# Edges sorted by destination block and source group, seven-chunk picks, and ranks made by TensorE, in a four-layer graph network on one core

## The reference

```python
# layer 0, twice: relational messages, summed by destination
W = jnp.einsum('rb,bio->rio', a, V)                  # 20 types out of 8 bases
agg = segment_sum(x[src], dst * R + etypes, N * R).reshape(N, R, -1)
h = jnp.einsum('nri,rio->no', agg, W) + x @ w_loop + bias
# layer 1: sum of the sources' rows
out = segment_sum(x[src], dst, N)
# layer 2: two small networks on every edge; their results are summed at the
# destination (forward) and at the source (backward), then a third per node
flow_f = mlp(cat(x[dst], x[src], edge_attr));  total_f = segment_sum(flow_f, dst, N)
flow_b = mlp(cat(x[src], x[dst], edge_attr));  total_b = segment_sum(flow_b, src, N)
x = mlp(cat(total_f, total_b))
# layer 3: attention with 4 heads of 8, softmax over the edges of a destination
scores = (q[dst] * k[src]).sum(-1) / sqrt(8);  out = segment_softmax(scores) * v[src] ...
```

## Time and profile before

| | before |
|---|---|
| time, median of 3 runs | 4352.77 us (4341.38 to 4362.70) |
| profiled execution | span 3621.4 us; no whole time is recorded for it |
| median minus span | 731.4 us |
| TensorE / VectorE / GpSimd / ScalarE busy | 72% / 71% / 62% / 16% |
| mean TensorE clock granted | 0.801 of full |
| instructions | 58407 |

### The profile page before, as it was taken

One profiled execution on the slowest core, in us unless ns is written; L12 is line 12 of the kernel. 1 busy time (PEld: TensorE's weight loads), 2 busy tenths in 40 slices (PEclk: granted clock), 3 DMA queues, 4 the chain that ended last, 5 costly groups with the idle time before them and its releaser, 6 DMA issues. The chain is left out here.

```text
span 3621.4 us, 58407 instructions
## 1 busy us (share of the span) xinstructions
PE 2609.3 (72%) x19499; PEld 1755.0 (48%) x19499; DVE 2555.5 (71%) x7445; ACT 577.7 (16%) x1352; POOL 2259.7 (62%) x2253
## 2 busy tenths in 40 slices
PE   0600000999998999977889799999999967777751
PEld 0400000777776777764555466666666543333331
DVE  9400000998874988869999677777777559999987
ACT  0100000000001000000011122222222213333320
POOL 2777776877762777747777355555555357777750
PEclk9555555788885888878889799999999968888885
DMA  6300001111113111111111100000000011111120
GB/s 96 103 8 8 8 8 58 31 23 24 25 12 103 25 23 24 24 17 28 26 27 26 12 10 10 11 10 10 10 11 10 6 24 27 27 27 27 27 19 5
DMA packets 125028, 91.67 MB, mean 25 GB/s; under 512 B 59542, under 2 KB 110678, under 8 KB 124118
## 3 DMA queue, kind: packets, MB, share of 16 engines
q0 software_dynamic: 70912, 41.10, 7.7%
q1 hardware_dynamic: 53846, 46.89, 5.3%
HBM read 60.42 MB, written 27.41 MB: 24 GB/s over the span
## 5 line engine op out<-in xcount | busy, mean ns | idle before, releaser
L726 POOL DMA_INDIRECT rel_rows<-message_table,message_indices x640 | 684.8, 1070 | 285.3 <-issue 193.9
L1279 POOL DMA_INDIRECT flow_x<-node_table,flow_index x440 | 441.0, 1002 | 409.8 <-DVE flow_index L1294 300.8
L1416 PE MATMUL flow_acc_bwd<-flow_onehot_j,flow_by_q 128*128 128x512 bf16 x2640 | 573.2, 336 | 0.0
L789 DVE TENSOR_SCALAR rel_source_onehot<-rel_sources,node_numbers 128x384 bf16<-128x384 f16 x2000 | 511.1, 320 | 79.4 <-PE p_rel_picked L863 78.0
L387 POOL DMA_INDIRECT sorted_edges<-stage,sorted_row x416 | 405.0, 974 | 192.0 <-issue 126.6
L863 PE MATMUL p_rel_picked<-rel_source_onehot,rel_h_parts 128*96 128x384 bf16 x2000 | 483.2, 417 | 53.7 <-issue 53.3
L1644 POOL DMA_INDIRECT att_kv_rows<-kv_table,att_index x440 | 427.1, 971 | 141.1 <-issue 131.7
L863 PEld LDWEIGHTS p_rel_picked<-rel_source_onehot,rel_h_parts 128*96 128x96 bf16 x2000 | 315.0, 161 | 214.2 <-issue 69.7
L1029 POOL DMA_INDIRECT sum_rows<-node_table,src_indices x280 | 272.1, 972 | 103.1 <-issue 80.8
L658 PE MATMUL p_rel_terms<-ident,source_centred 128*128 128x128 f32 (+1 forms) x4 | 1.1, 434 | 454.4 <-DVE source_centred L644 454.4
L1063 DVE TENSOR_SCALAR sum_source_onehot<-sum_sources,node_numbers 128x512 bf16<-128x512 f16 x1000 | 305.6, 371 | 14.9 <-PE p_sum_picked L1115 14.7
(11 more groups left out here) (286 smaller groups left out, 4882.9 us busy)
## 6 DMA issues: line engine op xcount, KB each, us to landing
message_table<-message_rows SPq DMA_DIRECT2D x50, 320.0 KB, 2.2
rel_rows<-message_table,message_indices POOLq DMA_INDIRECT x640, 2.5
rel_sources<-source_rows SPq DMA_DIRECT2D x80, 96.0 KB
flow_x<-node_table,flow_index POOLq DMA_INDIRECT x440
att_kv_rows<-kv_table,att_index POOLq DMA_INDIRECT x440, 2.4
sorted_edges<-stage,sorted_row POOLq DMA_INDIRECT x416
sum_sources<-source_rows SPq DMA_DIRECT2D x40, 128.0 KB, 3.0
sum_rows<-node_table,src_indices POOLq DMA_INDIRECT x280, 2.3
```

What stands on the lines that cost most here:

```text
L726: pool.indirect_dma_start(out=rows[b][:, t, :], out_offset=None, in_=d["messages"], in_offset=bass.IndirectOffsetOnAxis(ap=s["idx_msg"][:, ...
L789: last = dve.tensor_scalar(which[g % 2][:, c, :], srcs[b][:], s["node"][:, c:c + 1], None, ALU.is_equal)
L1279: pool.indirect_dma_start(out=X[b][:, t, 0:F], out_offset=None, in_=d["nodes"], in_offset=bass.IndirectOffsetOnAxis(ap=ibuf[b][:, t:t + 1] ...
L1416: last = pe.matmul(accB[:, lo:hi], S[b][:, t, k, :], J[b][:, t, lo:hi], start=False, stop=True, skip_group_check=True)
```

## The change

The source nodes are cut into SG = 4 groups of GC = 7 chunks. Edges are sorted by destination block and, within it, by source group, and each of the 100 buckets is padded to whole tiles. T becomes 520. A tile's sources then lie in 7 known chunks.

- The picks compare with 7 chunks instead of 25. The group's first chunk comes from a second register read per group (`dcol` has four rows now), and each picked tile has its own products: RPT = 6 tiles of RG = 13 in the relational layers (one table, padded to 128 columns, is stationary; the one-hot moves), PT = 8 of 13 in the sum layer. There the one-hot is stationary, so the rows come out upright; the turning and one of the two copies are gone.
- In the relational layers the coefficients are bf16 products of three parts; the picks have one PSUM tile of two banks, which holds the coefficients too.
- Flow's backward sums go to 256 columns at the group's place (JW), by one matmul; a read of four registers per group is added.
- The ranks come from TensorE. Products of a column's block one-hot and group one-hot give the counts; beside the scatters, for every 8 columns, `edge_places` turns the block one-hots, multiplies them with themselves, VectorE masks the result to "lower partition", and two more products give each edge's place. GpSimd waits for the rows of each 8 columns.
- SyncE's queue writes the padding (from 52 tiles' worth of it, repeated) ahead of the edge attributes. `tile_maps` takes the place of `block_limits`.

The diff, cut to its core:

```diff
-T = ((E - NB) // P + NB + BUFS * G - 1) // (BUFS * G) * (BUFS * G)
+SG, GC = 4, 7
+GW = GC * P
+BUCKETS = NB * SG
+T = ((E + (P - 1) * BUCKETS) // P + BUFS * G - 1) // (BUFS * G) * (BUFS * G)
-QJ = (NB // 4) * P + LAST
+JW = 2 * P
-            "dcol": sb(ctx, "dst_columns", [1, 2, T], I32),
+            "dcol": sb(ctx, "tile_columns", [1, 4, T], I32),
...
 # sort_edges, SyncE
+                    sp.wait_ge(recs, 2)
+                    sp.dma_start(d["sorted"][0:T * P, :]..., s["rec"][:, 0:FILL, :]...
+                                 .to_broadcast([P, T // FILL, FILL * REC])).then_inc(pads, 16)
                     sp.dma_start(stage[:, 0:FULL, 0:FE], a["edge_attr_16"][whole, :]...)
...
 # sort_edges, GpSimd
+                    pool.wait_ge(records_staged, 3)
+                    pool.wait_ge(staged, 64)
+                    pool.wait_ge(pads, 16)
                     for c in range(EC):
+                        if c % SUB == 0:
+                            pool.wait_ge(order["ready"], c // SUB + 1)
                         pool.indirect_dma_start(
...
+def edge_places(...):
+        def turn(k):
+            for c in range(SUB):
+                last = pe.transpose(pT[k % 2][0:NB, c * P:(c + 1) * P], hotb[:, k * SUB + c, :], s["identb"][:])
+        def compare(k):
+            for c in range(SUB):
+                x = turnedb[k % TURNED][:, c * P:(c + 1) * P]
+                last = pe.matmul(pE[k % 2][:, c * P:(c + 1) * P], x, x, start=True, stop=True)
+        def put(k):
+            for c in range(SUB):
+                pe.matmul(pR[k % 2][:, c], turnedb[...], top(first[:])[:, :, :, e], ...)
+                last = pe.matmul(pR[k % 2][:, c, 0], lower[k % 2][:, c, :], hots[:, e, :], ...)
+        def mask(k):
+            dve.tensor_tensor(lower[k % 2][:], pE[k % 2]..., below[:]..., ALU.mult).then_inc(masked, 1)
+        def rows(k):
+            # product, sum, cast, two integer steps, and the row: six instructions, each waited for
...
-RG, RPT, RBUFS = 11, 3, 6
+RG, RPT, RBUFS = 13, 6, 5
...
 # relational layers, TensorE
                     def pick(g):
                         pe.load(regs[g % 3], s["dcol"][0:1, 0, g * RG:(g + 1) * RG])
+                        pe.load(first, s["dcol"][0:1, 2, g * RG + RGT:(g + 1) * RG])
                         pe.wait_ge(which_ready, g + 1)
-                        for c in range(NB):
-                            last = pe.matmul(pp[g % 2][0:3 * F, 0:RW], hs[:, c]..., which[g % 2][:, c, :], ...)
+                        if g >= 1:
+                            pe.wait_ge(coef_taken, g)
+                        for t in range(RPT):
+                            at = pe.snap(first[t], min_val=0, max_val=(SG - 1) * GC)
+                            for c in range(GC):
+                                last = pe.matmul(pp[:, t * P:(t + 1) * P],
+                                                 hs[:]...[:, bass.ds(at * P + c * P, P)],
+                                                 which[g % 2][:, c, t * P:(t + 1) * P], ...)
...
                     def coefficients(g):
                         for t in range(RPT):
-                            last = pe.matmul(pc[...], kinds[g % 2][:, t * P:(t + 1) * P], ab[:], ...)
+                            for j in range(3):
+                                last = pe.matmul(pc[...], kinds[...], top(ab[:])[:, j, :], ...)
...
 # sum layer
-    G, PT, bufs = 11, 4, 4
+    G, PT, bufs = 13, 8, 4
+                        pe.load(first, s["dcol"][0:1, 2, g * G + GT:(g + 1) * G])
+                        for t in range(PT):
+                            at = pe.snap(first[t], min_val=0, max_val=(SG - 1) * GC)
+                            k, n = divmod(t, PT // 2)
+                            for c in range(GC):
+                                last = pe.matmul(pp[g % 2][:, k, n * 3 * F:(n + 1) * 3 * F],
+                                                 which[g % 2][:, c, t * P:(t + 1) * P],
+                                                 table[:, bass.ds(at * (3 * F) + c * 3 * F, 3 * F)], ...)
-                        turn(g)
-                        if g >= 1:
-                            picked_rows(g - 1)
                         gathered_rows(g)
+                        picked_rows(g)
...
 # flow layer
                         if products[0] == 0:
+                            pe.load(groups, s["dcol"][0:1, 3, bass.ds(g * G, G)])
                             pe.wait_ge(msg_ready, g + 1)
-                            for lo, hi in ((0, BANK), (BANK, QJ)):
-                                last = pe.matmul(accB[:, lo:hi], S[b][:, t, k, :], J[b][:, t, lo:hi], ...)
+                            last = pe.matmul(accB[:, bass.ds(back_col(t), JW)], S[b][:, t, k, :], J[b][:, t, :], ...)
```

589 lines of the change are left out of this document (348 added, 241 removed).

## The result

The changed kernel takes 5203.8 us (median of 4, 5185.8 to 5216.8) against 4348.1 us (median of 4): a ratio of 1.198, 95% interval 1.193 to 1.203. The forecast was slower by 2.2%; it is slower by 20%. The sign was right, and 856 us stand where 95 were forecast.

A forecast was written before the change was run, and what follows sets the result against it. Four loops of tile groups set the time, with TensorE and VectorE nearly full and gathers running all the time. Sorting +1, around loops +2, relational +40, sum +13, flow -75, attention +102, join +12: +95 on 4352.8, 4448 us; range 4315 to 4565.

The forecast's parts named there:

- The price of 12 us for ranks made beside the scatters: Sorting: new VectorE rank work slows the scatters by between 0 and 53 us; 12 us taken.
- The rival that they don't grow: Relational and sum loops: two register reads cost what one does, 2.3 us; whole kernel 4240 us, chance 0.14.
- The forecast's rule: Register reads: from a 16-byte multiple, four registers cost one access of some 0.25 us; otherwise each register costs 0.24.
- The pick is 42 products of 128 columns ... about 0.057 us: Relational group on TensorE: a pick takes 2.4 us at 2.4 GHz, 4.8 at 1.2; 3.9 taken.
- 56 x 0.043: Sum-layer group on TensorE: picks take 2.4 to 4.8 us, 4.1 expected, in a group of 10.1 us.
- Twelve save 2.9: TensorE 4.5 us. It no longer bounds: Flow group: narrower products cut TensorE to 4.5 us; group period taken as 5.7 us, flow -75 us.
- TensorE stays at 1.2 GHz: Rival for relational and sum loops: low clock throughout, 12.5 and 10.8 us a group, 4572 us; chance 0.12.
- every pick so far recovers: Argument against the rival of TensorE staying at 1.2 GHz: picks return to the high clock; that rival's chance 0.12.
- The 1.5 us that the forecast carried over: Relational pick: added for starting at the low clock, from 5.62 us against 4.23 before; pick taken as 3.9 us.
- if flow stays above 6.3: Flow loop: the prediction calls itself wrong if the group period stays above 6.3 us; it took 5.7.
- GpSimd has 4 x 1.27 = 5.1: Flow group: four gathers take 5.1 us on GpSimd, below the 5.3 us loop through VectorE's messages.
- The 731 us: Whole kernel: median 4352.8 us against profiled span 3621.4 us; 731 us said to lie around the span and stay.

## Why the prediction had the right sign and the wrong size

**Attention, join, sorting: right.** 65 groups at 10.45 us, where before had 55 at 10.24: +119 for +102. Join +11 for +12. First scatter at 66.8 for 66. The price of 12 us for ranks made beside the scatters was not paid: 416 scatters take 1.28 us each as before. That price, for work most of which "is short or reads PSUM", was the author's estimate, and no run shows it; from the first scatter to the last it is 531.2 us, where before had 530.7.

**The reads: right in length.** 3.1 and 1.1 us for 13 registers, 1.5 and 0.8 for 6, 4.0 us idle in a sum group (forecast 3.9). The rival that they don't grow is out. The forecast's rule was fitted to four times of before, and the reads of the runs keep to its counts. From a multiple of 16 bytes, what it counts as 1 to 5 accesses took 0.33 us (4 registers), 0.60 (8), 0.83 (6), 1.10 (13) and 1.32 (11); elsewhere 6 registers took 1.47 us, 8 took 1.94, 11 took 2.63 and 13 took 3.10. The traces show times alone: that accesses lie behind them is the author's reading. In a relational group the idle is 0.8 us, not 2.2: slower products lie ahead of the reads (basis products 4.0 us, forecast 2.1).

**"The pick is 42 products of 128 columns ... about 0.057 us" is the step that failed, with its twins, the sum layer's "56 x 0.043" and flow's "Twelve save 2.9: TensorE 4.5 us. It no longer bounds".** All three price a product by its columns alone. But these products have their address in a register plus an offset, and in the trace TensorE's queue has an operation for each of them: 3360 for 3360 relational picks, where 480 are left with the register taken as it is and none with constants. The four products of the sum layer's turning, from which the duration came, have fixed addresses, as have the picks of before, and the trace of before has no operation on their lines (L1132, L863). With an operation each, the picks start 0.124 us apart at either level of the clock: a relational pick takes 4.9 to 5.9 us, not 2.4 to 4.8, and a sum pick 7.6, not 2.4 to 4.8. In the sum layer that is the whole miss: with 8 of 56 operations left and the reads kept the group is at 10.2 us, the forecast 10.1. In flow, with 36 operations, TensorE bounds a group at 8.09 us instead of VectorE at 5.7; with 20, the group is at 6.33 us. The operations were in the trace of before too (2640 in flow, 24 a group, beside products of 821 columns), and the page counts them nowhere as busy.

**The clock was a rival, and it came true at a higher price.** "TensorE stays at 1.2 GHz" was given 0.12, at 12.5 and 10.8 us a group; it is at 0.62 and 0.50, with 14.9 and 14.6 us. The price lacked the operations. Its "every pick so far recovers" was argued from picks of before, which are 4 us of products of 384 columns; the new products start 0.124 us apart at the high level, where they start 0.056 us apart with constants. The 1.5 us that the forecast carried over for a pick that "starts low after the f32 products and the idle" come from one group: in the trace of before its pick has clock 0.50 from 811.6 to 813.6 us, but the pick at 663.42, behind the same products and 0.79 us of idle, has 1.00 throughout. Of the relational group's miss, message, basis and gathered products, which have no operation at the pick, hold 3.3 us over their terms, the picks 1.6, and the idle gives 1.4 back. The kernels tell the parts of the 5.1 us over fixed addresses apart only in part: halving the operations, or shortening the reads, gives back 2.8 us each, and each time the clock rises (0.69, 0.78). Both cannot count in full, as 5.6 is more than 5.1; no run has both. That short dense stretches hold the clock down was the author's estimate. The runs do not show the cause, only which clock went with which queue: the same products in the same order have 0.62 with the operations and both reads, 0.70 with one operation a tile, 0.78 with all operations but short reads, and 0.85 with neither operations nor the second read.

**Flow: wrong by 306 us, by two steps.** The forecast was -75 us, and it is +231. The forecast named its own test, "if flow stays above 6.3", and that is what happened. At least 229 us of it (130 x 1.76) go with 16 of the operations. The other failed step is "GpSimd has 4 x 1.27 = 5.1": once TensorE lets the gathers run on, they fall together with VectorE's products and stretch, and 4 of them take 6.3 to 6.7 us. That bound stands above the forecast's 5.7 even with operations fewer or gone.

**The 731 us: wrong, without effect.** They are not around the span. They belong to the longer executions and were in both kernels' times.

**The change as a whole.** With the new addresses constant it takes 3687 us, 54 us over before. The saved products and one-hots are then worth less than 80 more tiles cost in attention and join (130 us), because gathers hold the relational loops and flow. A kernel that also eases the gathers was not run.

## What to carry to other kernels

Count the instructions of a matmul's queue, not only its columns: here each pick at a register plus an offset had an operation (42 for 42 in a relational group) and the picks started 0.124 us apart, where from fixed addresses their 128 columns started 0.056 us apart at the high level and 0.107 at the low one. When an experiment frees one engine, look at what holds the new period before a price is worked out from it: with the addresses gone it was the gathers, in relational loops and in flow. When a change makes TensorE's work shorter and thinner, price the work that stays at the lower clock too: the relational loop had 0.62, where before had 0.81, and about half of a relational group's loss lay on lines without the new addresses. Put what a queue reads into registers at multiples of 16 bytes: 11 registers took 1.32 instead of 2.63 us, and that alone made the kernel before 0.5% faster.

## What the runs showed of the hardware

- **Time of one read by alignment.** 13 registers in 1.10 us at a multiple of 16 bytes, in 3.10 us elsewhere; 8 in 0.60 and 1.94 us, 6 in 0.83 and 1.47 us.
- **Gathers beside VectorE's products.** In flow a gather takes 0.94 us, and 2.6 us on the mean where it falls together with three products of 128x512 in bf16 that read two tiles (1.88 us); this is in the trace of the kernel with fixed columns in flow. The 391 that these products did not touch took at most 1.03 us.
- **Late completions.** In the longer executions, those in which before takes 4325 us, results reach other engines microseconds after TensorE's recorded end. From the changed kernel's first trace, attention, a timeline:

```profile
4506.38 1.03 PE L1913 MATMUL p_att_onehot<-identb,att_onehot 128*128 128x128 bf16 x8 [2.61 <-issue]
...
4508.91 0.60 PEld L1960 LDWEIGHTS p_att_sums<-att_messages,att_onehot 128*128 128x128 bf16 x16 [0.28 <-issue]
...
4510.22 0.14 PEld L1960 LDWEIGHTS p_att_sums<-att_messages,att_onehot 128*128 128x128 bf16 x2 [0.70 <-issue]
...
4511.76 1.01 ACT L1871 COPY att_onehot_turned<-p_att_onehot 128x1024 bf16<-128x1024 bf16 x1 [6.48 <-remote]
```

  ScalarE copies what TensorE has finished at 4507.4 only at 4511.8, and weight loads that followed each other at once come 0.7 us apart. In attention 35 of 64 periods are over 13 us by VectorE's products of messages and 60 by ScalarE's copies (4 by either in the shorter execution), and the mean is 16.3 us a group in the changed kernel and 16.5 in before, against 10.45 and 10.24. The scatters end later too (the last starts at 685 us, not 598), while the relational loops hardly differ in the changed kernel (15.3 against 14.8 us). In flow the mean period was 8.45 to 8.57 us in six such executions of the changed kernel and its variants, with 36 operations a group or 20. What holds TensorE in these executions is open; no kernel was made to find out, and the granted clock (0.65 in attention against 0.85) does not explain a wait of 4 us. One chip ran before in 4325 us and, eight minutes later, in 3631.
